# Attention block on one core: operand rows ordered by dimension then part, turned rows of the last three tasks copied by ScalarE

## The reference

```
q, k, v = split(x @ W_qkv.T); q, k = rope(q), rope(k)
scores  = q k^T / sqrt(8), causal
attn    = softmax(scores) @ v;   o = attn @ W_o.T
x1      = layernorm(x + o)
w       = int4-quantised ffn_kernel (one scale for the whole matrix)
out     = layernorm(x1 + x1 @ w + bias + (x1 @ a) @ b)
```

## Time and profile before

| | us |
|---|---|
| median of 3 runs | 459.44 |
| lowest and highest | 457.94, 460.96 |
| profiled execution, whole | 458.51 |
| its span in the trace | 456.7 |
| TensorE busy | 427.8 |
| VectorE busy | 382.5 |
| ScalarE busy | 314.6 |
| GpSimd busy | 119.3 |

### The profile page before, as it was taken

One profiled execution on the slowest core, in us unless ns is written; L12 is line 12 of the kernel. 1 busy time (PEld: TensorE's weight loads), 2 busy tenths in 40 slices (PEclk: granted clock), 3 DMA queues, 4 the chain that ended last, 5 costly groups with the idle time before them and its releaser, 6 DMA issues.

```text
span 456.7 us, 8431 instructions
## 1 busy us (share of the span) xinstructions
PE 427.8 (94%) x3198; PEld 207.8 (46%) x3198; DVE 382.5 (84%) x497; ACT 314.6 (69%) x637; POOL 119.3 (26%) x188
## 2 busy tenths in 40 slices
PE   6989798799999999999999999999999999999872
PEld 2547344345334444455444534444354445534541
DVE  3878699789999999989889999999898988843576
ACT  2554675476478687777878788868887888779720
POOL 8979401100210210030222302021002002341653
PEclk9999999799999999999999999999999999999995
DMA  7422211110000001110000011100000000000001
GB/s 242 162 94 93 96 44 52 55 52 32 2 2 0 3 28 55 55 54 10 3 2 1 4 55 55 54 33 1 1 1 2 1 3 2 2 3 24 16 10 46
DMA packets 11575, 16.55 MB, mean 36 GB/s; under 512 B 1820, under 2 KB 6700, under 8 KB 11536
## 3 DMA queue, kind: packets, MB, share of 16 engines
q1 hardware_dynamic: 10448, 15.75, 9.6%
q0 software_dynamic: 1088, 0.28, 0.4%
HBM read 10.37 MB, written 5.24 MB: 34 GB/s over the span
## 4 chain that ended last, share of the span: by engine, by line
PE 76%; DVE 8%; issue 5%; ACT 4%; POOL 4%; DMA 2%; POOLq 0%; DVEq 0%; ACTq 0%
PE oP L1219 26%; PE sT L1204 23%; PE ring L1157 15%; DVE pmax L980 7%; ACT probs L909 4%; PE sT L1125 3%; PE ring L1228 2%; POOL rstd L791 1%; PE ring L1171 1%; PE oP L1125 1%; DMA qS<-mrows 1%; POOL probs L816 1%; PE ring L1167 1%; DVE cs L1066 1%; PE ring L1181 1%
## 5 line engine op out<-in xcount | busy, mean ns | idle before, releaser
L980 DVE TENSOR_REDUCE pmax<-ring 128x2 f32<-128x1024 f32 (+3 forms) x273 | 318.8, 1216 | 35.5 <-PE ring L1157 26.6
L909 ACT ACTIVATE probs<-sT 128x512 f32<-128x512 f32 (+1 forms) x552 | 275.8, 587 | 89.6 <-PE sT L1204 87.7
L1204 PE MATMUL sT<-qS,kS 64*128 64x512 f32 (+3 forms) x616 | 177.1, 419 | 3.5 <-DMA qS<-mrows 1.9
L1219 PE MATMUL oP<-probs,vP 128*9 128x512 f32 (+3 forms) x1296 | 145.3, 529 | 2.8 <-POOL probs L816 2.7
L1157 PE MATMUL ring<-kS,qS 64*128 64x512 f32 (+3 forms) x640 | 142.8, 412 | 3.9 <-DVE pmax L980 1.6
L1204 PEld LDWEIGHTS sT<-qS,kS 64*128 64x128 f32 x616 | 86.1, 186 | 96.5 <-ACT probs L909 81.4
L1157 PEld LDWEIGHTS ring<-kS,qS 64*128 64x128 f32 x640 | 68.7, 186 | 44.0 <-DVE pmax L980 26.4
L816 POOL TENSOR_SCALAR_AFFINE_SELECT probs<-probs 128x512 f32<-128x512 f32 x64 | 40.3, 636 | 170.4 <-ACT probs L909 170.3
L825 POOL DMA_DIRECT2D qS<-mrows x34 | 19.6, 579 | 121.0 <-DVE mrows L1000 120.8
L1219 PEld LDWEIGHTS oP<-probs,vP 128*9 128x9 f32 x1296 | 20.7, 88 | 48.1 <-issue 29.2
L1171 PEld LDWEIGHTS ring<-causal_x,ident_x 64*128 64x128 f32 x188 | 18.3, 186 | 0.0
(11 more groups left out here) (132 smaller groups left out, 220.7 us busy)
## 6 DMA issues: line engine op xcount, KB each, us to landing
qS<-q_parts SPq DMA_DIRECT2D x52, 64.0 KB
kS<-k_parts SPq DMA_DIRECT2D x52, 64.0 KB
cs<-rope_tables_dram SPq DMA_DIRECT2D x4, 512.0 KB, 6.7
q_parts<-qp SPq DMA_DIRECT2D x4, 512.0 KB, 2.9
k_parts<-kp SPq DMA_DIRECT2D x4, 512.0 KB, 2.8
x_sb<-in_L_attn_x_dram SPq DMA_DIRECT2D x4, 256.0 KB, 5.9
out_dram<-rot SPq DMA_DIRECT2D x2, 256.0 KB, 2.3
qS<-mrows POOLq DMA_DIRECT2D x30, 8.0 KB, 2.1
```

The costliest lines, as they stand in the source:

```text
L909: nc.scalar.activation(probs[:, J % PRING, heads[0]:heads[-1] + 1:2, lo:hi], score_bank(at)[:, 0:len(heads) * (hi - lo)].rearrange("p (h s ...
L980: nc.vector.tensor_reduce(dst, src, AX.X, ALU.max).then_inc(unit_free, 1)
L1204: last = nc.tensor.matmul(score_bank(at)[:, x * w:(x + 1) * w], kS[rows, b, j // TPC, hp, (j % TPC) * TOK:(j % TPC + 1) * TOK], qS[rows, b ...
L1219: last = nc.tensor.matmul(oP[VW * h:VW * h + VC, lo:hi], vP[:, j, HG * g + h, :], probs[:, J % PRING, h, lo:hi], start=j == 0, stop=j == T ...
```

## The change

Three things change. First, the 32 operand rows of a head are no longer numbered part, part, dimension but part, dimension, part: `pick` is filled in the other order, and a load's DRAM side has the eight dimensions outermost and the two parts inside. Size and number of the loads stay. Second, for tasks 14 to 16 the copies behind POST 2 and POST 4 are made by ScalarE instead of VectorE. Third, three entries of the order's model change: `LANDING` 3.6 to 4.0, RSTD 0.45 to 1.2, and the copies by ScalarE get their own costs.

```diff
+LATE = range(TASKS.index((NG - 1, 1, 0, TPC)), len(TASKS))
+def copied_by_act(e):
+    return e[0] == "POST" and e[1] in LATE and e[2] in (2, 4)
...
-    LANDING = 3.6
+    LANDING = 4.0
...
-                self.pool = at = max(self.pool, ready) + 0.45
+                self.pool = at = max(self.pool, ready) + 1.2
...
                 if w == 0:
-                    of = dram[c, a, :, rows, :].rearrange("x (d h) s -> x d (h s)", h=PAIRS).to_broadcast([PARTS, DK, PAIRS * CH])
+                    of = dram[c, a, :, rows, :].rearrange("x (d h) s -> d x (h s)", h=PAIRS).to_broadcast([DK, PARTS, PAIRS * CH])
                 else:
-                    of = dram[c, :, 0, rows, :].rearrange("a (d h) s -> a d (h s)", h=PAIRS)
+                    of = dram[c, :, 0, rows, :].rearrange("a (d h) s -> d a (h s)", h=PAIRS)
...
-                            to = pick[:, w, a, hp, at:at + ROWS].rearrange("p (a x d) -> p a x d", a=PARTS, x=PARTS)
+                            to = pick[:, w, a, hp, at:at + ROWS].rearrange("p (a d x) -> p a x d", a=PARTS, x=PARTS)
...
+            def copy_turned(n, k):
+                e, i, (lo, hi) = ("POST", n, k), turn(n)[0], queries(n)
+                act.wait_ge(unit_done, UNIT[e])
+                nc.scalar.copy((onT if k == 2 else x1T)[i][:, lo:hi], ring_bank(e)[:, lo:hi]).then_inc(turned_copied, 1)
             for e in SCHEDULE:
+                if copied_by_act(e):
+                    copy_turned(*e[1:])
...
-                if e[0] == "POST":
+                if e[0] == "POST" and not copied_by_act(e):
                     post(*e[1:])
```

More of the change, by code:

```diff
@@ L304, in take @@
             at = self.dve
-            if kind == "POST":
+            if copied_by_act(event):
+                self.act = at = max(self.act, self.whole(0.55 * share, ready) + 0.25) + 0.14 + 0.43 * share
+                self.side = (self.side[0] + 0.55 * share, self.side[1])
+                self.ring = self.ring[1:] + (self.act + self.TO_PE,)
+            elif kind == "POST":
                 self.aside((0.55 if k in (2, 4) else 1.0) * share, (0.69 if k in (2, 4) else 2.0) * share, ready)
@@ L554, in attention_block @@
         rows_done = sem("rows_done")
+        turned_copied = sem("turned_copied")
         slots_set = sem("slots_set")
@@ L612, in attention_block @@
         for e in SCHEDULE:
-            if e[0] in RING_EVENTS:
+            if copied_by_act(e):
+                RELEASE[UNIT[e]] = (turned_copied, 1 + sum(s is turned_copied for s, _ in RELEASE.values()))
+            elif e[0] in RING_EVENTS:
                 RELEASE[UNIT[e]] = (rows_done, PARTS * (e[1] + 1)) if e[0] == "M" else (unit_free, 1 + sum(s is unit_free for s, _ in RELEASE.values()))
```

## The result

| | before | after |
|---|---|---|
| median, us (22 runs each) | 459.85 | 456.64 |
| lowest and highest | 456.90, 461.59 | 455.09, 460.74 |
| ratio after / before | | 0.9946 (0.9927 to 0.9966) |
| mean granted clock, median of the runs | 0.979 | 0.978 |

The kernel became 0.54% faster, about 2.5 us; forecast were 4.8. (The medians lie 3.2 us apart: 15 of the 22 runs after took 455.1 to 457.4 us, the other seven 459.2 to 460.7 with clocks of 0.967 to 0.972.) Two numbers of each run tell more than its time: its span, and its mean granted TensorE clock. Part of it is in the end of the program, where TensorE rests anyway: behind the last product with the values it is 4.6 us in the profile of before, 3.1 in that of after, and 2.6 to 6.3 in those of the experiments.

A forecast was written before the change was run, and what follows sets the result against it. TensorE was taken to bound 100 to 430 us, then the normalisation chain of three tasks the end. Terms -3.6 + 0.6 - 0.3 - 0.5 - 0.95 = -4.75, rounded -4.8, took 459.44 to 454.6 us; 8-in-10 range 451.5 to 459.3.

The forecast's parts named there:

- The loads and the wait: Task 2's first S: maxima rows land in 2.1 us instead of 4.4, and TensorE's 1.93 us wait goes.
- the two effects of the loads' shape: q and k loads on eight engines: shorter queues against more chances to hold the maxima back; which wins was left open.
- So I take it that the clock holds.: Behind task 2's wait: despite a hole grown from 0.7 to 1.2 us, no clock fall; 3.2 us of TensorE loss go.
- Rival 2: Wait at task 2 goes but the clock falls all the same: gain 3.1, so 456.3 us; chance 0.17.
- The order in the middle: +0.6.: Full TensorE stretch: ten more changes between row-split and whole-array matmuls cost 0.6 us, bounds 0 and +1.3.
- rival 3: Task 11: thinner filler between M and first S opens a wait if landings stay late; +3.6, 463.0 us; chance 0.10.
- The end: Copies and order of the last tasks: three terms of -0.3, -0.5 and -0.95 us.
- (a): At 424.85: TensorE's 0.58 us wait for task 13's first normalisation shrinks; -0.3 us, 0 to -0.6.
- (b): At 432.91 and 438.02: waits of 0.72 and 0.19 go, POST 2 of task 15 costs 0.38; together -0.5 us.
- (c): Behind the last product: five copies leave VectorE, 15.8 us shrink to 14.85; -0.95 us, 0 to -2.3.

The follow-up runs named there:

- e1: The kernel before with only the new order of the operand rows (`pick` and loads), the order of all engines unchanged; 456.94 us, ratio 0.9938.
- e4: The changed kernel with the old order of the operand rows, its order of all engines kept; 457.15 us, ratio 0.9939 to before.
- e8: The kernel before with repeated score matmuls filling TensorE's wait for the maxima rows of task 2, same values written; 457.96 us, ratio 0.9950.
- e12: e5 with one repeated score matmul pair each ahead of task 1's last mask wait and the turn of task 2's output; 451.27 us, ratio 0.9818.
- e5: The changed kernel with LANDING set back to 3.6, so the order up to task 13 is that of before; 452.84 us, ratio 0.9853.
- e11: e5 with the products of steps 5 and 6 of task 1 moved ahead of M of task 2; 455.50 us, ratio 0.9898 to before.
- e7: The kernel before with the new operand rows and LANDING 4.0, VectorE's copies and the old RSTD entry kept; 461.00 us, ratio 1.0025.
- e9: The changed kernel with the order of LANDING 3.6 up to event 310 (some 150 us), its own order behind; 453.90 us, ratio 0.9870 to before.
- e3: The kernel before with only LANDING 4.0 and RSTD 1.2, so a new order with old rows and VectorE's copies; 459.74 us, ratio 1.0023.
- e2: The kernel before with only the copies behind POST 2 and POST 4 of tasks 14 to 16 on ScalarE, old order; 458.46 us, ratio 0.9987.

## Why the prediction went wrong

*The loads and the wait.* Right. The rows of task 2 land in 2.0 to 2.2 us and those of task 5 in 1.9 to 2.1 (task 11 still has a 3.7, which nothing waits for), the wait is gone, and with the order of before (e1) this is worth 2.9 us, where -3.6 was forecast for wait and clock. Of the two effects of the loads' shape that were left open, the shorter backlog won.

*"So I take it that the clock holds."* This step failed. It rested on one window, 50 to 55 us, busy 3.76 of 5 with the clock at 1.00. In the trace of before it holds; in the profiles of the changed kernel and of all twelve experiments the clock is 0.66 to 0.84 in that very window. The profiled execution of before had a mean clock of 0.982; of 67 runs of before timed beside e4, e8 and e12 only 7 reached that, and their median is 0.979. I took a lucky execution for the rule. The fall at 50 to 55 us is not itself what the change lost, for e5 and e12, the fastest, have it too; what it took away is the ground for trusting 80 to 95 us. There the hole that I saw grow from 0.7 to 1.2 us brings the clock down (e11: 2.1 to 2.7 us), though the changed kernel's own profile has one fall ahead of it as well. And M does move, against the forecast: VectorE waits for it, 0.51 us at the low clock and 0.29 in e11 at the full one. Rival 2 named the mechanism, but at one place and at 3.2 us, and not that it differs from run to run. Its number, 456.3, is 0.3 from the measured median; that is luck, as the order cost more than it says and the end gave more.

*"The order in the middle: +0.6."* Failed too. The whole of the order that LANDING 4.0 makes costs about 4 us beside the new rows (e5: 3.8, e7: 4.1): the larger part ahead of 150 us, with the clock, and about 1 us behind it (e9) as rest of TensorE. This I had put as changes of array mode; it is waits, 1.0 us for VectorE's maxima and 0.4 for ScalarE's exponentials, in a stretch where I had counted on none. I looked for M of task 11 as the place of danger (rival 3); nothing waits for maxima rows there, with landings of 3.7.

*The end.* Mechanism right, terms (a), (b) and (c) too small: -2.1 for the first two against -0.8, and -1.8 for the third against -0.95. The order alone gives the first (e3). The three waits that (a) and (b) name are 0.58 + 0.72 + 0.19 = 1.5 us, and they all went: TensorE rests 0.2 us in this stretch where it rested 1.7. I took only 0.3 for the first of them, and charged 0.38 for POST 2 of task 15. The remaining 0.6 is shorter busy time for the same work, which no run explains. Of the third, ScalarE's copies give 0.8 in the old order (e2). In the new one they and their entries in the model, which change the last 37 events again, give 1.6 behind the last product (15.6 in e3, 14.0 after) and take 0.4 ahead of it: 1.1 together. That copies and order help each other is not shown by so little.

*The sum.* Rows -2.9, middle order about +4, end about -3.9: together -2.8, measured -2.5. Without the middle order it is -6.8, and e5, which leaves just that out, gained 6.8. With the old rows the parts do not add: the middle order would cost 3.8 by e3 and 1.1 by e4, by the ratios and the ends in their traces.

## What to carry to other kernels

In a stretch where two engines are nearly level, judge an order by the holes that it leaves on TensorE, not only by what it waits for: moving filler from behind a short wait to ahead of it cost four to five times the wait's growth of 0.5 us, through the clock. Read the granted clock of many runs before calling a place safe; one profile is one draw. And when a change bundles a transfer, a copy and a planner's constant, time each with the others held, since one of them may be eating what the others earn.

## What the runs showed of the hardware

- The same kernel's clock falls in some executions and not in others: e11 has three runs at 0.971 and three at 0.979 to 0.985, with times of 456.6 to 456.8 and 453.4 to 454.4.
- Matmuls that compute nothing new paid for themselves in e8 (2.2 us, clock loss 10.8 to 7.5) and probably in e12 (1.6 us, intervals overlapping). The Trainium skill, TensorE: Matmul & The Clock Gate, section "Part 1: The HAM clock gate", says that the clock follows how busy TensorE has been recently; e8, whose only change is that work, agrees with it: 1.00 at 85 to 90 us, where before had 0.57.
- The new loads keep the DMA engines busy for longer with the same bytes. At 80 to 85 us the DMA share is 0.24 of 16 engines at 70 GB/s, so 3.8 engines' time and 18 GB/s for each; before it is 0.15 at 56, 2.4 engines' time and 23 GB/s for each. Over the whole program the queue of SyncE's transfers takes 10.8% of the engines' time instead of 9.6% for the same 15.75 MB. Issuing a load on SyncE took longer as well, 652 ns against 591.
- A small transfer's landing depends on what loads run beside it: the same rows of task 2 take 2.1 and 4.4 us before, 1.9 and 2.2 in e1, which changes only the shape of the loads.
